# Softmax over the neighbours moved from one block over all batches into the batches of the neighbour sum

## What is computed

```python
h = lrelu(_bn(feat @ W1.T, g1, b1))
h = lrelu(_bn(h @ W2.T, g2, b2))
h = lrelu(_bn(h @ W3.T, g3, b3))          # _bn: mean and variance over batches, points and neighbours
att = jax.nn.softmax(h[..., 0], axis=-1)  # over the 30 neighbours
xk = x.transpose(0, 2, 1)[bidx, idx]
agg = jnp.einsum('bnkc,bnk->bnc', xk, att)
return x + agg.transpose(0, 2, 1)
```

## Time and profile before

| | us |
|---|---|
| median of 3 runs | 6845.02 (6840.62 to 6846.48) |
| profiled execution | 6844.73 |
| its span | 6842.6 |
| span up to 5018 (attention and neighbours) | 5018.0 |
| 5018.0 to 5518.4 (batch norms, three layers) | 500.4 |
| 5518.4 to 5567.6 (softmax over all batches) | 49.2 |
| 5567.6 to the end (neighbour sum) | 1275.0 |

### The profile page before, as it was taken

The page is one execution under the profiler, slowest core; times in us unless marked ns, Lnnn a source line. Parts: engine busy times, 40 slices in busy tenths (PEclk is TensorE's granted clock), DMA queues, the critical chain, the costliest instruction groups (busy, mean ns, idle before and its releaser), DMA issues. The chain is left out here.

```text
span 6842.6 us, 225161 instructions
## 1 busy us (share of the span) xinstructions
PE 5734.9 (84%) x83284; PEld 3508.2 (51%) x83284; DVE 6094.3 (89%) x8460; ACT 4453.1 (65%) x17048; POOL 4826.1 (71%) x4750
## 2 busy tenths in 40 slices
PE   7888888888888888888888888888849949899998
PEld 3444544444454545454445544554523337666666
DVE  7999999999999999999999999999956588777776
ACT  7777777777777777777777777777732533233223
POOL 6788888888888888888888888888860013333332
PEclk9998889888898898898888988989859979999999
DMA  1222222222222222222222222222232013323322
GB/s 35 76 84 80 78 72 78 78 72 72 94 74 78 84 80 76 74 78 74 76 72 90 78 78 80 84 72 78 68 105 50 0 35 90 82 80 85 83 80 76
DMA packets 378892, 509.44 MB, mean 74 GB/s; under 512 B 288876, under 2 KB 302444, under 8 KB 343820
## 3 DMA queue, kind: packets, MB, share of 16 engines
q1 hardware_dynamic: 377740, 494.03, 24.0%
HBM read 378.46 MB, written 65.14 MB: 65 GB/s over the span
## 5 line engine op out<-in xcount | busy, mean ns | idle before, releaser
L673 ACT ACTIVATE prob<-SC,row_max 128x64 f32<-128x64 f32 x6144 | 1831.0, 330 | 649.6 <-DVE row_max L1019 642.8
L790 POOL TENSOR_TENSOR k_bd<-k_t,head_mask 128x512 f32<-128x512 f32 x1536 | 1629.5, 1082 | 8.2 <-POOL dist_row L768 4.5
L673 ACT ACTIVATION_READ_ACCUMULATOR prob<-SC,row_max 128x1 f32 x6144 | 1368.1, 223 | 0.0
L1003 DVE FIND_INDEX8 nbr<-top,dist 128x8 uint16<-128x1024 f32 x1024 | 1235.3, 1218 | 0.0
L999 DVE MAX8 top<-dist 128x8 f32<-128x1024 f32 x1024 | 1193.3, 1206 | 12.3 <-DVE y_b L1042 9.9
L801 POOL TENSOR_TENSOR prob<-prob,row_rec 128x512 f32<-128x512 f32 x768 | 830.1, 1081 | 468.2 <-DVE row_rec L1027 468.2
L584 PE MATMUL PT<-ident,prob 128*128 128x128 f32 x3072 | 541.5, 305 | 513.7 <-ACT prob_t L680 510.8
L563 PE MATMUL SC<-k_bd,q_t 128*64 128x256 f32 x6144 | 939.0, 432 | 0.0
L1001 DVE MATCH_REPLACE8 dist<-top,dist 128x1024 f32<-128x1024 f32 x768 | 924.0, 1207 | 0.0
L584 PEld LDWEIGHTS PT<-ident,prob 128*128 128x128 f32 x3072 | 403.9, 157 | 1007.7 <-issue 990.4
L1801 DVE TENSOR_TENSOR d_oh_a<-lo,iota_a 128x4096 bf16<-128x4096 bf16 x256 | 583.9, 2291 | 278.4 <-PE DM L1653 277.8
(11 more groups left out here) (195 smaller groups left out, 10848.0 us busy)
## 6 DMA issues: line engine op xcount, KB each, us to landing
low_all<-low_scratch SPq DMA_DIRECT2D x256, 1024.0 KB, 5.0
placed<-compact SPq DMA_DIRECT2D x256, 192.0 KB, 3.8
ctx<-in_ctx SPq DMA_DIRECT2D x32, 512.0 KB, 4.1
mask<-in_mask SPq DMA_DIRECT2D x32, 512.0 KB, 7.4
xb<-in_x SPq DMA_DIRECT2D x32, 512.0 KB, 4.8
x_scratch<-xb SPq DMA_DIRECT2D x32, 512.0 KB, 4.8
y_scratch<-y_b SPq DMA_DIRECT2D x32, 512.0 KB, 6.7
d_x<-x_scratch SPq DMA_DIRECT2D x32, 512.0 KB, 5.1
```

What stands on the lines that cost most here:

```text
L673: last = act.activation(prob[:, s % 4, g * CHUNK:(g + 1) * CHUNK], SC[:, s % 2, g * CHUNK:(g + 1) * CHUNK], ACT.Exp, bias=row_max[:, s % 2 ...
L790: last = pool.tensor_tensor(k_bd[:, q % KEY_BUFS, ch, :].rearrange("p (h k) -> p h k", h=8), kk, hm, ALU.mult)
L1003: last = dve.max_index(nbr[:, uu % BPB, t, k * 8:(k + 1) * 8], best, row)
```

## The change

The block over all batches goes. In `batch_norms` GpSimd now lays the third layer's raw values out as `att`, pair by pair, behind each transpose; gain and shift of the third layer are kept in tiles of their own (`gain3`, `shift3`). In `neighbour_sum` ScalarE's copy into at_n applies gain and shift; VectorE takes the leaky ReLU, maximum and difference of the next batch at t=3 (`exponents`) and one_hot_blocks behind it; ScalarE takes the exponent behind x=8 (`powers`); VectorE takes sum, reciprocal and product at t=4 ahead of the transpose (`weights`). `moments_of` moves from t=4 to t=5, while the read of the sum's second half stays at t=4, and the normalisation moves from x=13 to x=15. At the start of the stage the first batch's weights come ahead of clearing `placed`, on GpSimd and VectorE.

```diff
+                if n == 1:
+                    by_row = att[:, :, :].rearrange("p (b t) k -> p b t k", t=NT)
+                    for m in range(PAIRS_K):
+                        pool.wait_ge(z3_turned, m + 1)
+                        pool.tensor_copy(by_row[:, :, :, 2 * m:2 * m + 2], S[:, 0, 2 * m:2 * m + 2, :].rearrange("p k (t b) -> p b t k", t=NT)).then_inc(laid_out, 1)
+            pool.wait_ge(laid_out, PAIRS_K)
...
-            wait(act, "gain3")
-            act.wait_ge(z3_turned, PAIRS_K)
-            by_row = S[:, 0, :, :].rearrange("p k (t b) -> p b t k", t=NT)
-            for x in range(PARTS_S):
-                mine = att[:, x * SHARE:(x + 1) * SHARE, 0:K].rearrange("p (b t) k -> p b t k", t=NT)
-                share = SHARE // NT
-                act.activation(mine, by_row[:, x * share:(x + 1) * share], ACT.Identity, scale=gain[2][:, 0:1],
-                               bias=shift[2][:, 0:1]).then_inc(u3_ready, 1)
-            for x in range(PARTS_S):
-                mine = att[:, x * SHARE:(x + 1) * SHARE, 0:K]
-                act.wait_ge(lowered, x + 1)
-                act.activation(mine, mine, ACT.Exp).then_inc(powered, 1)
...
-            wide = [128, SHARE, K]
-            dve.memset(att[:, :, K:KP], 0.0)
-            for x in range(PARTS_S):
-                own = slice(x * SHARE, (x + 1) * SHARE)
-                dve.wait_ge(u3_ready, x + 1)
-                link(dve.scalar_tensor_tensor(att[:, own, 0:K], att[:, own, 0:K], SLOPE, att[:, own, 0:K], ALU.mult, ALU.max))
-                link(dve.tensor_reduce(top[:, own], att[:, own, 0:K], AX.X, ALU.max))
-                dve.tensor_tensor(att[:, own, 0:K], att[:, own, 0:K], top[:, own].unsqueeze(2).to_broadcast(wide), ALU.subtract).then_inc(lowered, 1)
-            for x in range(PARTS_S):
-                own = slice(x * SHARE, (x + 1) * SHARE)
-                dve.wait_ge(powered, x + 1)
-                link(dve.tensor_reduce(total[:, own], att[:, own, 0:K], AX.X, ALU.add))
-                link(dve.reciprocal(total[:, own], total[:, own]))
-                dve.tensor_tensor(att[:, own, 0:K], att[:, own, 0:K], total[:, own].unsqueeze(2).to_broadcast(wide), ALU.mult)
+            wait(dve, "gain3")
...
                 act.wait_ge(at_ready, START + b(1))
-                act.activation(at_n[:, :].rearrange("p (n k) -> p n k", k=KP), keep["att"][:, bass.ds(b(NT), NT), :],
-                               ACT.Identity).then_inc(copied_in, 1)
+                act.activation(at_n[:, :, 0:K], keep["att"][:, bass.ds(b(NT), NT), :], ACT.Identity, scale=keep["gain3"][:, 0:1],
+                               bias=keep["shift3"][:, 0:1]).then_inc(copied_in, 1)
+
+            def powers(b):
+
+
+                act.wait_ge(lowered, START + b(1, 1))
+                act.activation(at_n[:, :, 0:K], at_n[:, :, 0:K], ACT.Exp).then_inc(powered, 1)
 
...
                     if x == 1 and not is_last(i, u):
                         weights(counter(i, u + 1))
-                    if x == 13 and not is_first(i, u):
+                    if x == 8 and not is_last(i, u):
+                        powers(counter(i, u + 1))
+                    if x == 15 and not is_first(i, u):
                         normalise(counter(i, u - 1), (u - 1) % BPD)
 
             weights(counter(0, 0))
+            powers(counter(0, 0))
             all_batches(act, body)
...
+            split_weights(counter(0, 0), 0, False)
             pool.memset(placed[:, 1, :, :, :, :], 0.0).then_inc(cleared[1], 1)
-            split_weights(counter(0, 0), 0, False)
             all_batches(pool, body)
...
-            dve.wait_ge(consts_in, START + 16 * len(CONSTS))
...
+            def exponents(b):
+
+
+                own, wide = at_n[:, :, 0:K], [128, NT, K]
+                dve.wait_ge(copied_in, START + b(1, 1))
+                dve.scalar_tensor_tensor(own, own, SLOPE, own, ALU.mult, ALU.max).then_inc(leaky, 1)
+                dve.wait_ge(leaky, START + b(1, 1))
+                dve.tensor_reduce(top[:, :], own, AX.X, ALU.max).then_inc(highest, 1)
+                dve.wait_ge(highest, START + b(1, 1))
+                dve.tensor_tensor(own, own, top[:, :].unsqueeze(2).to_broadcast(wide), ALU.subtract).then_inc(lowered, 1)
+
             def weights(b):
-                dve.wait_ge(copied_in, START + b(1, 1))
+                own, wide = at_n[:, :, 0:K], [128, NT, K]
+                dve.wait_ge(powered, START + b(1, 1))
+                dve.tensor_reduce(total[:, :], own, AX.X, ALU.add).then_inc(scaled, 1)
+                dve.wait_ge(scaled, START + b(3, 1))
+                dve.reciprocal(scale[:, :], total[:, :]).then_inc(scaled, 1)
+                dve.wait_ge(scaled, START + b(3, 2))
+                dve.tensor_tensor(own, own, scale[:, :].unsqueeze(2).to_broadcast(wide), ALU.mult).then_inc(scaled, 1)
+                dve.wait_ge(scaled, START + b(3, 3))
                 dve.wait_ge(at3_ready, START + b(1))
-                dve.transpose(at_t[:, :], at_n[:, :]).then_inc(at_ready, 1)
+                dve.transpose(at_t[:, :], at_n[:, :, :].rearrange("p t k -> p (t k)")).then_inc(at_ready, 1)
...
             def moments_of(b, u):
-                read_sum(b, u, 1)
                 dve.wait_ge(read_out, START + b(2, 2))
...
                     if t == 2 and not is_last(i, u):
                         indices(counter(i, u + 1), (u + 1) % BPD)
                     if t == 3 and not is_last(i, u):
+                        exponents(counter(i, u + 1))
+                        one_hot_blocks(counter(i, u + 1))
+                    if t == 4 and not is_first(i, u):
+                        read_sum(counter(i, u - 1), (u - 1) % BPD, 1)
+                    if t == 4 and not is_last(i, u):
                         weights(counter(i, u + 1))
-                    if t == 4 and not is_first(i, u):
+                    if t == 5 and not is_first(i, u):
                         moments_of(counter(i, u - 1), (u - 1) % BPD)
-                    if t == 5 and not is_last(i, u):
-                        one_hot_blocks(counter(i, u + 1))
                     if t >= 6 and not is_last(i, u):
                         compact_blocks(counter(i, u + 1), i, (u + 1) % BPD, t - 6)
 
+            dve.memset(at_n[:, :, K:KP], 0.0)
+            indices(counter(0, 0), 0)
+            exponents(counter(0, 0))
+            dve.wait_ge(consts_in, START + 16 * len(CONSTS))
+            one_hot_blocks(counter(0, 0))
+            weights(counter(0, 0))
             dve.memset(placed[:, 0, :, :, :, :], 0.0).then_inc(cleared[0], 1)
-            indices(counter(0, 0), 0)
-            weights(counter(0, 0))
-            one_hot_blocks(counter(0, 0))
             for h in range(2):
                 compact_blocks(counter(0, 0), 0, 0, h)
             all_batches(dve, body)
             first_half(BODY_D - 1, BPD - 1)
+            read_sum(counter(BODY_D - 1, BPD - 1), BPD - 1, 1)
             moments_of(counter(BODY_D - 1, BPD - 1), BPD - 1)
```

More of the change, by code:

```diff
@@ L1127 @@
 LOADS = (0, 4, 12, 20, K)
-PARTS_S = 4
-SHARE = N * NT // PARTS_S
 BN_ROW = (("W1", 36), ("W2", 18), ("W3", 3), ("g1", 6), ("g2", 3), ("g3", 1), ("b1", 6), ("b2", 3), ("b3", 1))
@@ L1184, in batch_norms @@
         inv = sb("inv", [128, 2])
-        gain = [sb(f"gain{n}", [128, w]) for n, w in ((1, 2), (2, 1), (3, 1))]
-        shift = [sb(f"shift{n}", [128, w]) for n, w in ((1, 2), (2, 1), (3, 1))]
-        top = sb("top", [128, N * NT])
-        total = sb("total", [128, N * NT])
+        gain = [sb(f"gain{n}", [128, w]) for n, w in ((1, 2), (2, 1))] + [keep["gain3"]]
+        shift = [sb(f"shift{n}", [128, w]) for n, w in ((1, 2), (2, 1))] + [keep["shift3"]]
         Z = ps("Z", [128, BANKS, 512])
@@ L1209, in batch_norms @@
         u2_ready = sem("u2_ready")
-        u3_ready = sem("u3_ready")
-        lowered = sem("lowered")
-        powered = sem("powered")
+        laid_out = sem("laid_out")
         block = es.enter_context(nc.Block())
@@ L1494, in neighbour_sum @@
         iota_m = sb("iota_m", [128, 8], BF16)
-        at_n = sb("at_n", [128, NT * KP])
+        at_n = sb("at_n", [128, NT, KP])
+        top = sb("top", [128, NT])
+        total = sb("total", [128, NT])
+        scale = sb("scale", [128, NT])
         at_t = sb("at_t", [128, NT * KP])
@@ L1521, in neighbour_sum @@
         at_ready = sem("d_at_ready")
+        leaky = sem("leaky")
+        highest = sem("highest")
+        lowered = sem("lowered")
+        powered = sem("powered")
+        scaled = sem("scaled")
         at3_ready = sem("at3_ready")
@@ L1882, in build @@
         attention_and_neighbours(nc, dram, keep)
-        keep["att"] = es.enter_context(nc.sbuf_tensor("att_all", [128, N * NT, KP], F32))
+        keep["att"] = es.enter_context(nc.sbuf_tensor("att_all", [128, N * NT, K], F32))
+        for name in ("gain3", "shift3"):
+            keep[name] = es.enter_context(nc.sbuf_tensor(name, [128, 1], F32))
         batch_norms(nc, dram, keep)
```

## The result

| | us |
|---|---|
| before, median of 4 runs beside it | 6842.93 |
| after, median of 4 runs | 6902.94 (6902.58 to 6904.68) |
| ratio | 1.0088, 95% interval 1.0073 to 1.0102 |
| profiled execution of after, its span | 6900.8 |

The change makes the kernel slower by 60 us; 6890 (6855 to 6925) was predicted. On the way to the first DM it gains 58 us, and from there to the end it loses 116.5, of which 114.5 are in the 31 transitions between batches (each counted from one t=4 to the next) and 2.0 in batch 0 ahead of its t=4.

The account below looks back on a forecast made before the run. VectorE's path from t=4 to t=0 was taken as a second loop as long as TensorE's 35.05 us batch. Loss 2 + 17 x 4.5 + 13 x 2.0 = 104.5, gain 57.2, net +47 on 6844.73: 6890 us, range 6855 to 6925.

Parts of the forecast that it names:

- Removed, 49.2, and GpSimd's copies at 0: Ahead of the neighbour sum: the 49.2 us softmax block goes whole; 15 new GpSimd copies in the third layer cost 0.
- Start of the stage, 8: Start of the neighbour sum: first DM 20 to 21 us in, against 31.4; gain 6 to 11, taken as 8 us.
- The wait for the exponent, 1.95: At t=4 VectorE waits for ScalarE's exponent behind x=8: 1.95 us of new idle time per batch.
- The split and its wait, 2.2: GpSimd's split takes turns with d_oh_a at t=5 and t=6; VectorE idles another 2.2 us ahead of compact.
- The addition on the second group: GpSimd's d_y+d_x moves from the first compact group to the second, costing 2.16 us of VectorE time there.
- Rival 1: GpSimd's addition doesn't block VectorE in a critical place, so the DMA counts: net +17, 6862 us; chance 0.15.
- t=7 2.0 us late: In each batch's loop, TensorE's t=7 comes 2.0 us late because VectorE's d_oh_a is late.
- t=0 4.5 us late: At the next batch's t=0 in plain transitions, TensorE is 4.5 us late, the 2.0 at t=7 included.
- DMA gate: DMA from compact to t=0, 6.7 us: the other gate of t=0, giving at least +2.7 us there.
- The sum, 104.5: Loss over 31 transitions between batches: first 2, 17 plain at 4.5, 13 at a jump at 2.0; 104.5 us.
- Rival 3: TensorE's clock: new gaps lengthen AG behind them, 17 x 0.9 = 15 us more, 6905, up to 6925; chance 0.12.
- Rival 2: Split not held back, t=7 in time: net -43, 6802 us; gains below about 1.9 us per transition; chance 0.11.

Follow-up runs that it names:

- short addition: The changed kernel with GpSimd's addition d_y+d_x cut from 1024 to 64 columns: 6845.40 us, ratio to before 1.0003.
- short split: The changed kernel with GpSimd's split cut to its first cast, the other two parts of the weights left zero: 6831.12 us, ratio to before 0.9980.
- moments in the wait: The changed kernel with moments_of put back from t=5 to t=4, ahead of weights: 6901.44 us, ratio to before 1.0081.
- `powers` behind x=6: The changed kernel with ScalarE's exponent taken behind piece x=6 in place of x=8: 6839.84 us, ratio to before 0.9992.

## Why the prediction was right, and by how much it was off

- **Removed, 49.2, and GpSimd's copies at 0.** Both came as forecast.
- **Start of the stage, 8.** Measured 8.5 (22.8 us against 31.4); with the block it is 58.3, predicted 57.2. The memset didn't hold the split back, but the first DM wasn't 20 to 21 us in, as worked out for that case: VectorE's own memset stands ahead of compact in its order, so compact starts at 5532.79, where the split had ended at 5530.58. The 8 that was taken, from the middle of 6 to 11, met the measured value by luck in part.
- **The wait for the exponent, 1.95.** 1.93; t=5 starts 6.40 us behind t=4, predicted 6.39.
- **The split and its wait, 2.2.** 2.35. The casts were 2.38, 2.70 and 0.61: one meets t=5, one t=6, one nobody, as worked out from batch 0.
- **The addition on the second group.** 4.06 us for that group, with the addition started at 6336.18. Rival 1, by which it wouldn't block VectorE in a critical place, is refuted.
- **t=7 2.0 us late.** The waits at t=5 and t=7 are 0.26 + 1.72 = 1.98.
- **t=0 4.5 us late.** From t=2's start it is 27.89 us, and was 23.18: 4.71. The DMA gate of 6.7 us, the lower bound, doesn't bind: with the short addition t=0 waits 0.24 us for d_oh_a.
- **The sum, 104.5.** 116.5. Here the forecast was off, by terms of opposite sign. The 17 plain transitions cost 92.1 us in place of 76.5 (5.42 each in place of 4.5): the AG behind the gap is longer (0.75 in the transition shown), and XT, DM and t=0 come a little later too. The 13 at a jump cost 18.8 in place of 26 (1.45 each in place of 2.0), in line with the stalls at the jumps that are 5.9 shorter in all. The first transition cost 3.6 in place of 2. And batch 0, which the sum doesn't have, is 2.0 longer up to its t=4 (11.45 us behind the first DM, 9.46 before): TensorE has no AG there to hold VectorE back, so the steps at t=3, which the prediction called free, aren't free in this one batch. 104.5 + 15.6 - 7.2 + 1.6 + 2.0 = 116.5.
- **Rival 3.** Its mechanism is there, on every plain transition; the prediction gave it 0.12 and left it out of the sum. It should have been a term of it: the earlier trace rows showed the longer AG behind a long gap, and the earlier trace rows a gap of 1.01 with a DM of 2.56, unlengthened. That the forecast still came near (6890 against 6903) is in part luck, since the jumps cost less than they were put at.
- **Rival 2, not slower.** Its limit, that the change gains when a transition costs less than 1.9 us, was right: each kernel that takes away one wait or the addition comes to 0.2% of before or closer. From the first DM on they lose 53, 44.5 and 57 us, over 30 transitions 1.8, 1.5 and 1.9 each. Of the three only the short split is clearly faster than before (0.9971 to 0.9990).

## What to carry to other kernels

Work of a stage that is moved into a loop as "free" steps must have its partners' answers at the place where its engine asks for them: count back from each wait to the instruction that ends it, and put the step one tile earlier rather than filling the wait with other work. A chain of short GpSimd steps beside long two-input VectorE instructions runs at one step for each of them; the single-input instructions between those are its room, so moving them away lengthens the chain. And a gap on TensorE is to be priced above its length: by about a third where a gap was all that was added (11.8 on 34.9, 5.6 on 18.3), but by anything from 7.8 on 49.3 (short addition) to 44.6 on 71.6 (moments in the wait) in the kernels above, since it depends on what the lower clock falls on.

## What the runs showed of the hardware

The lower clock of an AG behind a single gap doesn't grow evenly with the gap. With `powers` behind x=6, gaps of 2.77 or 2.78 us were followed by an AG of 4.10 to 5.39 in nine cases and of 3.74 to 3.92 in three others.

In the changed kernel's plain transitions, with a gap of 1.4 to 1.7 us at t=7, the AG is even shorter behind a longer gap at t=0: 4.65 to 5.31 behind four gaps of 1.72 to 1.96, 4.25 to 4.59 behind twelve of 2.05 to 2.35, and 4.00 behind one of 2.58. The longer gap lets more of the low stretch pass before the AG begins: in the transition shown, the clock is at 1.2 GHz from 6342.62 to 6346.03, and the AG that starts at 6344.51 has 1.52 us of it (3.68 + 0.76 = 4.44, measured 4.43).
